# Keeping the last four blocks of a mixture of experts, not two, out of the sums in DRAM

## The reference

```python
logits = x @ gate_w                               # 2048 tokens, 8 experts
mult, sel = _sparse_mixer_routing(logits)         # two experts and two weights for each token
w = jnp.sum(mult[:, :, None] * (sel[:, :, None] == jnp.arange(E)[None, None, :]), axis=1)
h = jax.nn.silu(jnp.einsum('th,ehf->etf', x, w1)) * jnp.einsum('th,ehf->etf', x, w3)
out = jnp.einsum('etf,efh,te->th', h, w2, w)
...
x = _layernorm(x + _L0_ffn_ref(x, ...), axis=-1)
return x
```

## Time and profile before

| | us |
|---|---|
| median of 3 runs | 675.57 (674.59 to 675.78) |
| profiled execution | 674.35 |
| its span, first to last instruction | 672.7 |
| TensorE busy in the span | 580.6 (86%) |
| VectorE busy | 455.6 (68%) |
| ScalarE busy | 247.8 (37%) |
| GpSimd busy | 285.6 (42%) |
| mean granted TensorE clock | 0.935 of full speed |

### The profile page before, as it was taken

One profiled execution on the slowest core, in us unless ns is written; L12 is line 12 of the kernel. 1 busy time (PEld: TensorE's weight loads), 2 busy tenths in 40 slices (PEclk: granted clock), 3 DMA queues, 4 the chain that ended last, 5 costly groups with the idle time before them and its releaser, 6 DMA issues.

```text
span 672.7 us, 13915 instructions
## 1 busy us (share of the span) xinstructions
PE 580.6 (86%) x3498; PEld 452.7 (67%) x3499; DVE 455.6 (68%) x1363; ACT 247.8 (37%) x475; POOL 285.6 (42%) x208
## 2 busy tenths in 40 slices
PE   6999989699698867556998989999999999999940
PEld 2444568588366645444786878888888888888840
DVE  2566487956567778967775757768677777677751
ACT  3555540001676633224222414242332242422333
POOL 7100020002093447646651856719484185761142
PEclk9999999999889979557999989999999999999985
DMA  8999507201300106222367574856767467444453
GB/s 272 330 335 336 181 1 202 51 1 44 144 2 1 34 24 251 79 92 92 80 166 189 148 197 98 241 128 160 201 156 219 94 144 220 82 94 88 77 165 122
DMA packets 75514, 93.15 MB, mean 138 GB/s; under 512 B 15837, under 2 KB 70494, under 8 KB 72656
## 3 DMA queue, kind: packets, MB, share of 16 engines
q1 hardware_dynamic: 63808, 78.81, 40.0%
q0 software_dynamic: 6768, 9.32, 7.4%
q10 hardware_dynamic: 4896, 4.53, 2.7%
HBM read 42.67 MB, written 31.67 MB: 111 GB/s over the span
## 4 chain that ended last, share of the span: by engine, by line
PE 60%; DVE 17%; POOL 7%; ACT 5%; issue 5%; DMA 4%; SPq 1%; another core or an unknown queue 1%; ACTq 0%; POOLq 0%; DVEq 0%
PE bank L2382 23%; PE bank L2394 12%; PE bank L1952 8%; PE bank L2111 4%; POOL experts_w L859 2%; DVE region L1374 2%; DVE region L1372 2%; DMA xcol<-xcol 1%; PE bank L2002 1%; PE bank L1961 1%; ACT wstage L1242 1%; DVE small L1391 1%; PE bank L1968 1%; DMA wstage<-total 1%; PE bank L2279 1%
## 5 line engine op out<-in xcount | busy, mean ns | idle before, releaser
L2382 PE MATMUL bank<-experts_w,experts_x 128*128 (+1 forms) x864 | 216.9, 401 | 3.9 <-issue 3.9
L2382 PEld LDWEIGHTS bank<-experts_w,experts_x 128*128 128x128 f32 x864 | 158.2, 189 | 38.3 <-issue 5.1
L2394 PEld LDWEIGHTS bank<-experts_w 128*128 128x128 f32 x840 | 105.2, 191 | 5.1 <-issue 2.3
L2394 PE MATMUL bank<-experts_w 128*128 x840 | 106.3, 283 | 1.7 <-DVE region L1857 1.7
L907 POOL DMA_INDIRECT total<-region,rid x34 | 52.6, 1547 | 125.4 <-DVE region L1857 103.4
L1172 ACT ACTIVATE region<-bank 128x512 f32<-128x512 f32 x72 | 42.3, 597 | 129.7 <-PE bank L2382 119.4
L1833 DVE TENSOR_TENSOR xcol<-region,bank 128x512 f32<-128x512 f32 x72 | 49.1, 682 | 40.6 <-ACT region L1172 40.5
L778 POOL TENSOR_TENSOR small<-small 128x4 f32<-128x4 f32 (+5 forms) x20 | 25.7, 1288 | 102.9 <-DVE small L1383 84.1
L1178 ACT CAST experts_w<-bank 128x512 fp32r<-128x512 f32 x70 | 40.6, 587 | 72.3 <-DVE bank L1842 65.4
L1952 PE MATMUL bank<-xcol,region 128*128 128x512 f32 x128 | 58.8, 618 | 7.4 <-DMA xcol<-in_xT 5.8
L887 POOL TENSOR_TENSOR experts_w<-wstage,experts_w 128x2048 f32 x12 | 55.3, 4624 | 13.2 <-ACT experts_w L1196 13.2
(11 more groups left out here) (367 smaller groups left out, 914.8 us busy)
## 6 DMA issues: line engine op xcount, KB each, us to landing
wstage<-in_w_exp SPq DMA_DIRECT2D x18, 1024.0 KB, 5.2
xcol<-xcol SPq DMA_DIRECT2D x140, 128.0 KB
slots<-padrow SPq DMA_DIRECT2D x8, 2210.0 KB, 19.8
wstage<-in_w_exp SPq DMA_DIRECT2D x2, 3072.0 KB, 12.1
region<-slots ACTq DMA_DIRECT2D x34, 130.0 KB
xcol<-in_xT SPq DMA_DIRECT2D x4, 512.0 KB, 6.7
xtok<-in_x SPq DMA_DIRECT2D x1, 2048.0 KB, 13.1
region<-in_ctxT SPq DMA_DIRECT2D x1, 2048.0 KB, 8.0
```

Source lines behind the costliest of these rows:

```text
L2382: mm = pe.matmul(bank[2 * u + m][:, :], (xTh, xTl)[a][:, s, k, :], moving(off, w, m * KD * F + k * F + u * HALF, HALF), start=(k == 0 and ...
L2394: mm = pe.matmul(bank[into][:, 0:D], (high, low)[a][:, u, c, :], moving(off, w, 2 * KD * F + (4 * u + c) * D, D), start=(u == 0 and c == 0 ...
```

## The change

Four blocks, g - 2 to last, are kept out of the sums (`LATE`). So that all four are the last expert's, the number of its blocks is set to at least four; the others are then filled with empty rows. Reading `total` back depends only on the send of block g - 3. The reading of part 0 is issued by ScalarE inside its `last_pair`, that of the others by SyncE. GpSimd's `last_pair` has no sends and has four gathers, into four more tiles of `ya`. The statistics, shifts and norms of the first parts are written into the last pair of VectorE and ScalarE. The down product of g - 1 goes to bank 7 and that of last to bank 3, as banks 6, 7, 1 and 3 hold the four late products until they are added. Two more rows of weights and row numbers are kept (`weight_end`, `rid_end`), and the tiles of the small statistics have room for NT + LATE entries. At the end GpSimd sends the rows of four blocks in place of two. ScalarE's `high_up(g)` in the last pair is gone (no new expert can begin there).

```diff
-ENDS = ((0, 2), (2, 4), (6, 4), (10, 4), (14, 2))
+ENDS = ((0, 4), (4, 4), (8, 4), (12, 2), (14, 2))
+LATE = 4
...
-        ya = wstage[:, 0:NT * D].rearrange("p (i d) -> p i d", d=D)
+        ya = wstage[:, 0:(NT + LATE) * D].rearrange("p (i d) -> p i d", d=D)
...
```

SyncE (`sp`):

```diff
-            for s in range(2):
-                sp.wait_ge(y_sent[s], 8 * even + 16 * s)
-                sp.sem_inc(sp_gate, 1)
+            sp.wait_ge(y_sent[1], 8 * even)
+            sp.sem_inc(sp_gate, 1)
...
-            for u, (first, n) in enumerate(ENDS):
+            for u in range(1, len(ENDS)):
+                first, n = ENDS[u]
                 sp.dma_start(ya[:, first:first + n, :], rows_of(total, u)).then_inc(y_back[u], 16)
...
-            sp.wait_ge(rows_sent, 16 * 2)
+            sp.wait_ge(rows_sent, 16 * LATE)
```

GpSimd (`pool`):

```diff
-            all_pairs(pool, pair, pair)
-            last = pool.value_load(tab_n[0:1, 1:2], min_val=2 * SURE - 2, max_val=NB - 2) + 1
-            pool.wait_ge(xg_turned, last + 1)
-            pool.sem_inc(pool_gate, 1)
-            pool.wait_ge(meta_done, last + 1)
-            pool.sem_inc(pool_gate, 1)
-            pool.wait_ge(y_sent[1], 8 * (last + 1))
-            pool.sem_inc(pool_gate, 1)
-            pool.wait_ge(rid_end_done, 1)
-            for s in range(2):
-                pool.indirect_dma_start(out=xg[:, s, 0:D], out_offset=None, in_=total,
-                                        in_offset=bass.IndirectOffsetOnAxis(ap=rid_end[:, s:s + 1], axis=0)).then_inc(gathered[s], 16)
+            def last_pair(p):
+                pool.wait_ge(y_sent[1], 16 * p)
+                pool.sem_inc(pool_gate, 1)
+                pool.wait_ge(rid_end_done, 1)
+                for n in range(LATE):
+                    pool.indirect_dma_start(out=ya[:, NT + n, :], out_offset=None, in_=total,
+                                            in_offset=bass.IndirectOffsetOnAxis(ap=rid_end[:, n:n + 1], axis=0)).then_inc(gathered[n], 16)
+            all_pairs(pool, pair, last_pair)
             for first, n in ENDS:
                 rsqrt(n, first)
-            rsqrt(2, NT)
+            for k in range(0, LATE, 2):
+                rsqrt(2, NT + k)
             pool.wait_ge(out_done, 16 * len(ENDS))
-            pool.wait_ge(fin_done, len(ENDS) + 1)
-            for s in range(2):
-                pool.indirect_dma_start(out=out, out_offset=bass.IndirectOffsetOnAxis(ap=rid_end[:, s:s + 1], axis=0),
-                                        in_=xg[:, s, 0:D], in_offset=None, bounds_check=T - 1,
+            for n in range(LATE):
+                if n % 2 == 0:
+                    pool.wait_ge(fin_done, len(ENDS) + n // 2 + 1)
+                pool.indirect_dma_start(out=out, out_offset=bass.IndirectOffsetOnAxis(ap=rid_end[:, n:n + 1], axis=0),
+                                        in_=ya[:, NT + n, :], in_offset=None, bounds_check=T - 1,
                                         oob_is_err=False).then_inc(rows_sent, 16)
```

ScalarE (`act`):

```diff
+            def norm_rows(u, first, n, ends):
+                act.wait_ge(shift_done, u + 1)
+                for k in range(first, first + n):
+                    row = ya[:, k, :]
+                    ins = act.activation(row, row, ACT.Identity, bias=shift[:, k:k + 1], scale=rsy[:, k:k + 1])
+                if ends:
+                    ins.then_inc(fin_done, 1)
             def last_pair(p):
                 g = 2 * p
+                last = g + 1
                 for u in range(2):
                     silu(g, u)
+                act.wait_ge(y_sent[1], 8 * g)
+                act.sem_inc(act_gate, 1)
+                first, n = ENDS[0]
+                act.dma_start(ya[:, first:first + n, :],
+                              total[first * P:(first + n) * P, :].rearrange("(i p) d -> p i d", p=P)).then_inc(y_back[0], 16)
                 for u in range(2):
                     high_turned(g - 1, u)
-                high_up(g)
-                last = g + 1
                 silu(last, 0)
                 act.wait_ge(grouped[0], 32 * g + 64)
                 act.sem_inc(act_gate, 1)
                 plain(last, 0)
                 for u in range(2):
                     high_turned(g, u)
+                norm_rows(0, 0, 4, True)
                 silu(last, 1)
                 high_end(0)
                 plain(last, 1)
+                norm_rows(1, 4, 3, False)
                 high_end(1)
+                norm_rows(1, 7, 1, True)
             all_pairs(act, pair, last_pair)
-            for u, (first, n) in enumerate(ENDS):
-                act.wait_ge(shift_done, u + 1)
-                for k in range(first, first + n):
-                    row = ya[:, k, :]
-                    ins = act.activation(row, row, ACT.Identity, bias=shift[:, k:k + 1], scale=rsy[:, k:k + 1])
-                ins.then_inc(fin_done, 1)
...
+            for u in range(2, len(ENDS)):
+                norm_rows(u, *ENDS[u], True)
+            for k in range(0, LATE, 2):
+                norm_rows(len(ENDS) + k // 2, NT + k, 2, True)
```

VectorE (`dve`); the first line is in the building of the block tables, after L1763:

```diff
+            link(dve.tensor_scalar(nblk[:, E - 1:E], nblk[:, E - 1:E], float(LATE), None, ALU.max))
...
+            waiting = {}
+            def end_stats(u):
+                first, n = ENDS[u]
+                dve.wait_ge(y_back[u], 16)
+                waiting[u] = norm_stats(first, n, 1e-5, first, ya)
+            def end_shift(u):
+                first, n = ENDS[u] if u < len(ENDS) else (NT + 2 * (u - len(ENDS)), 2)
+                n = slice(first, first + n)
+                dve.wait_ge(rs_done, waiting[u])
+                dve.scalar_tensor_tensor(shift[:, n], mv[:, n, 0], -1.0, rsy[:, n], ALU.mult, ALU.mult).then_inc(shift_done, 1)
+            def keep_end(n, of):
+                dve.tensor_scalar(weight_end[:, n:n + 1], of[:, 1:2], 1.0, None, ALU.mult)
+                return dve.tensor_scalar(rid_end[:, n:n + 1], of[:, 0:1], 1.0, None, ALU.mult)
+            def late_rows(g, n, down_in):
+                dve.wait_ge(down_done, 2 * g + 2)
+                dve.wait_ge(gathered[n], 16)
+                link(dve.scalar_tensor_tensor(ya[:, NT + n, :], bank[down_in][:, 0:D], weight_end[:, n:n + 1], ya[:, NT + n, :],
+                                              ALU.mult, ALU.add))
             def last_pair(p):
                 g = 2 * p
                 last = g + 1
                 rows(last, 1)
                 middle(g, 0, 0)
-                keep_meta(g - 1, 1)
+                dve.wait_ge(meta_kept, g - 1)
+                keep_end(0, kept[:, 0])
+                dve.wait_ge(meta_done, g + 1)
+                keep_end(1, meta[:, 1, 3:5])
                 row_meta(last, 1)
+                keep_end(2, meta[:, 0, 3:5])
+                dve.wait_ge(meta_done, last + 1)
+                keep_end(3, meta[:, 1, 3:5]).then_inc(rid_end_done, 1)
                 middle(g, 0, 1)
...
-                weigh(g - 2, 0)
+                end_stats(0)
                 middle(last, 1, 0)
-                keep_meta(g, 0)
-                dve.wait_ge(meta_done, last + 1)
-                dve.tensor_copy(rid_end[:, 0:1], meta[:, 0, 3:4])
-                dve.tensor_copy(rid_end[:, 1:2], meta[:, 1, 3:4]).then_inc(rid_end_done, 1)
...
-                weigh(g - 1, 1)
+                end_shift(0)
+                end_stats(1)
                 middle(last, 1, 1)
-                keep_meta(last, 1)
-                for u in range(2):
-                    low_turned(last, u, bank[2 * u], endTh, endTl)
+                low_turned(last, 0, bank[0], endTh, endTl)
+                end_shift(1)
+                end_stats(2)
+                low_turned(last, 1, bank[2], endTh, endTl)
+                end_shift(2)
+                end_stats(3)
+                end_stats(4)
+                end_shift(3)
+                late_rows(g - 2, 0, 6)
+                late_rows(g - 1, 1, 7)
+                end_shift(4)
+                waiting[5] = norm_stats(NT, 2, 1e-5, NT, ya)
+                late_rows(g, 2, 1)
+                late_rows(last, 3, 3)
+                end_shift(5)
+                waiting[6] = norm_stats(NT + 2, 2, 1e-5, NT + 2, ya)
+                end_shift(6)
             all_pairs(dve, pair, last_pair)
-            for u in range(len(ENDS) + 2):
-                if u < len(ENDS):
-                    first, n = ENDS[u]
-                    dve.wait_ge(y_back[u], 16)
-                    norm_stats(first, n, 1e-5, first, ya)
-                elif u == len(ENDS):
-                    whole_rows(last - 1, 0, 1)
-                    whole_rows(last, 1, 6)
-                    norm_stats(0, 2, 1e-5, NT, xg)
...
```

TensorE (`pe`), in `last_pair`:

```diff
-                    down(g - 1, u, off, hTh, hTl)
+                    down(g - 1, u, off, hTh, hTl, 7)
...
-                    down(last, u, off, endTh, endTl, 6, g)
+                    down(last, u, off, endTh, endTl, 3)
```

More of the change, by code:

```diff
@@ L225, in decoder_kernel @@
         padrow = sb("padrow", ROW)
-        small = sb("small", 1017)
+        small = sb("small", 1037)
         at = [0]
@@ L249, in decoder_kernel @@
```

(28 more changed lines are left out.)

22 lines of the change are left out of this document (5 added, 17 removed).

## The result

The changed kernel takes 669.83 us (median of 13 runs, 665.50 to 672.14); the kernel before, over 13 runs beside it, 675.62 (670.36 to 677.19). The ratio is 0.9912, 95% interval 0.9892 to 0.9933: faster by 5.8 us, where 5.5 had been forecast (670.1). The profiled execution has a span of 668.6 us, against 672.7. Of all timed executions in this document one is left out as slow: 700.95 us at a clock of 0.814, of block_first, whose other three took 661.55 to 667.29 us.

A forecast was written before the change was run, and what follows sets the result against it. Bound: 26 us behind TensorE's end, set by the first read, the two engines' order and the sends. End 667.1 plus 0.17 gave span 667.3 against 672.7, 5.4 less; median 670.1 us, range 668.9 to 671.7.

The forecast's parts named there:

- The bound: End of the kernel: 26 us come after TensorE ends, and work there could lie beside TensorE, where VectorE and ScalarE have room.
- Start of the read: ScalarE in the last pair: block 31's sum lands at 628.95 us, and the first part's read is issued at 629.
- T: Landing of the first four tiles of `total`, when VectorE's statistics start: 634.1 us, bounds 632.9 and 635.7.
- the regrouping of block 34: SP's four copies before the last transposes: issued by 632.1 us, due at 636.65.
- The starving: Rival: block 34's regrouped rows land late, at 641.0 us for +4.3, or after 11.8 us for 677.4; chance 0.07.
- Every microsecond of T is one of the end: Crowding rival's rule: VectorE and ScalarE stand in line from T to X; T 637.2 gives end 3.1 later; chance 0.21.
- The two lines from there to X: VectorE and ScalarE in the last pair: four norms to 641.7 us, SiLU to 642.3, last low part to 646.75.
- X: End of the last low part, block 35: 646.75 us, 2.06 later than before, with TensorE ending near 648.4.
- Writes and sends: Kernel's end: last tiles written at 655.1 us (3.22), span ending 9.3 after plus two more sends at 1.36: 667.1.
- Signs of being wrong: T past 637; SP's parts issued before the regrouping lands and holding it; GpSimd's late powers (0.7 to 1.0 us) holding a shift.
- The sum: Whole kernel: span 667.3 us against 672.7, 5.4 less, and median 670.1; chance 0.55.
- the longer table chain: Start of the kernel: one more linked VectorE operation in the table chain, taken as +0.17 us.

The follow-up runs named there:

- block_first: Changed kernel with block 35's work ahead of the closing layernorm on VectorE and ScalarE; ratio to the kernel before 0.9878, tail 42.9 us.
- all_behind: Changed kernel with VectorE's statistics and shifts and ScalarE's norms of the 16 tiles behind the last pair again; tail 47.8 us.
- gathers_later: Changed kernel with GpSimd's four gathers waiting until block 34 has been transposed; tail 47.2 us.
- regroup_clear: block_first plus GpSimd's first power ahead of its gathers and SyncE's reads waiting for block 34's regrouping; 665.51 us, ratio to the kernel before 0.9896, tail 41.7.
- read_later: Changed kernel with ScalarE issuing the first part's read behind its two copies of block 33's turned rows; tail 44.1 us.
- two_sends: Changed kernel with GpSimd sending only the rows of blocks 34 and 35, leaving out 32 and 33; tail 41.8 us.
- bulk_later: Changed kernel with SyncE's reads of parts 1 to 4 waiting until block 34 has been transposed; tail 44.3 us.

## Why the prediction was right

**The bound.** That the 26 us behind TensorE were the place to gain, and that VectorE had room for a part of that work beside TensorE, held: with the statistics put back (all_behind) the tail is 47.8, with them 42.6.

**Start of the read and T.** 3.9 and 8.9 us after block 31's send were predicted, 3.8 and 9.0 came. The estimate between two bounds was good (5.2 us from issue to use for 0.52 MB). By the fit of the Trainium skill (DMA: Bandwidth & Descriptors, Anatomy of one DMA) it would be 3.2, an estimate for a transfer alone, and the page has the fit from transfers that GpSimd issues, while ScalarE issues this one; the measurement decides. Yet T hardly mattered, as it had 1.7 us of slack. SyncE's reads began at 10.4 (9.0 in the two other profiles), not at 6.9. Its last issue of the regrouping ends at 632.98 and its first read starts at 636.41; what it does in between stays open.

**The step that was mis-sized: the regrouping of block 34.** I had its landing due at 11.5 and not late; it landed at 13.4, 7.05 us from the start of the last issue. In the kernel before it was there by 10.2, as the transposes ran without a wait. The starving that stood among the rivals did occur, at 2.0 us instead of the 4.3 to 7.3 priced there (both prices run from 632.1, the end of the last issue; the 8.86 us of the earlier trace rows run from an issue's start, and the last one starts at 631.5, so they are 0.6 too high). The reads do it together: gathers away 0.3 to 0.9, SyncE's parts away 0.3, both away 1.5 or more. The Trainium skill (DMA: Bandwidth & Descriptors, Queues, rings and completion order) has all queues share the same engines in turn, and the runs agree: the copies, issued on SyncE's queue before its own reads, land 7.05 us from the start of their last issue, 6.20 when GpSimd's gathers come later (gathers_later), and at most 5.6 when SyncE's reads do too (regroup_clear). Whether its second half, the order of completion, adds to that, no run here separates. What the first read alone costs wasn't tried, as there was no run without it. Where nothing was altered ahead of it this landing still differs by up to 0.5 us (transposes at 13.5, and at 14.0 in block_first), so the single shares are no better than that. "Every microsecond of T is one of the end" was wrong in its subject: read_later gave 1.5 for 3.4. There the transposes' start and the tail both moved by 1.5. In regroup_clear 1.4 at the transposes gave 0.9.

**The two lines from there to X.** With the transposes 2.0 late, the SiLU came 1.8 and X 1.5 late: the steps between were a little shorter than summed. From X to the last tiles' shift the prediction takes 4.06 and 3.91 came (649.15 to 653.06); its own terms there add up to 3.89 (0.09, twice 1.13, 0.09, 1.30 and 0.15), so the terms were right and the addition was 0.17 too long.

**Writes and sends.** Here the error was given back. The first send starts 3.2 us after ScalarE's last norm of the tiles (28.1 to 31.4), where 4.1 had been summed from the 3.22 of the earlier trace rows and 0.86. The write lands 2.1 us after its issue, not 3.2, and it isn't what GpSimd waits for any more: that is VectorE's line through the late blocks, which the prediction had taken as covered. Sends follow each other by 1.27 to 1.36, where 1.36 was taken. The third send starts 1.5 us after the last late norms (32.5 to 34.0), where 2 had been summed, and a send needs 0.93 of that behind the norms (two_sends); so the added sends cost 0.7 to 0.8 in their own right though they stand on the path with 2.6.

**Signs of being wrong.** The prediction named three. The first, T past 637, didn't come. The second did: SyncE's parts are issued at 10.4, before the regrouping lands at 13.4, and bulk_later puts their hold at 0.3 us. The third did too: VectorE's last shift stands 0.81 us for GpSimd's late power (657.28; 0.75 in the kernel before, at 659.78), and the one of part 2 stands 0.24 (649.39). The time came out right although two of the prediction's own signs of being wrong were there; 0.3 and 0.81 us are small beside its range.

**The sum.** Tail 41.9 predicted, 42.5 measured: the gain in the tail is 4.97 us (47.51 less 42.54), not 5.6. The median moved by 5.8. What lies before the tail moves by more than this from run to run, so that the median agrees so closely is partly luck. For the same reason no run shows the 0.17 us taken for the longer table chain: the start of block 31's send alone differs by 5.3 us between two profiles of the changed kernel (626.06 and 620.77).

## What to carry to other kernels

When work is moved beside a busy engine, the order on the two helper engines becomes the path. Walk that line instruction by instruction, with every power or SiLU that one of them waits for: a wait of 5.37 us came out at the end with 4.6, while taking away one of 0.69 gained 0.1 to 0.2, as it uncovered the next (twice 0.53 us for GpSimd, then 1.39 for a write).

An early transfer isn't free because its own data come in time: look which transfers of the old critical work it runs beside. Here reads of up to 2.6 MB (20 tiles of 128 x 256) on three queues delayed 0.5 MB of copies that nobody had waited for before.

Undo the moved work and keep the early data: that one run showed which half of the change carried the gain.

## What the runs showed of the hardware

Three profiles of one and the same program spread over 5.2 us in span (668.6, 663.4, 666.5), while their tails agree within 0.1 (42.54, 42.63, 42.61). The difference lies in the middle of the program. Stages of the changed kernel's first profile, then of its second (columns as above):

```profile
100.00:200.00 100.00, 87.34 (x680) 65.72 (x680) 68.19 (x160) 25.95 (x63) 20.30 (x16) 0.91 0.26 75
...
300.00:340.00 40.00, 32.27 (x145) 25.85 (x146) 27.57 (x116) 11.51 (x11) 26.12 (x25) 0.79 0.28 84
...
400.00:620.00 220.00, 219.34 (x1259) 190.32 (x1258) 156.83 (x434) 75.95 (x105) 127.54 (x46) 1.00 0.62 152
```

```profile
100.00:200.00 100.00, 86.84 (x692) 65.80 (x691) 68.55 (x161) 26.76 (x66) 20.13 (x16) 0.95 0.26 75
...
300.00:340.00 40.00, 34.17 (x165) 27.45 (x165) 31.96 (x128) 13.89 (x15) 29.07 (x27) 0.85 0.37 97
...
400.00:620.00 220.00, 219.34 (x1260) 190.27 (x1259) 156.69 (x429) 76.48 (x106) 125.97 (x45) 1.00 0.61 149
```

From 400 us on both have a clock of 1.00 and the same busy time; between 100 and 200 us the granted clock is 0.91 in the one and 0.95 in the other, between 300 and 340 us 0.79 and 0.85. Such a mean lies between the two levels of 1.2 and 2.4 GHz: the clock was at the lower one for a larger or smaller part of the stretch. The mean over the span is 0.926, 0.943 and 0.936 in the three, and the one with the highest is the shortest. The 13 timed runs say the same: the four with a mean clock of 0.939 or more took 665.50 to 667.79 us, the other nine, at 0.933 or less, 669.16 to 672.14. That the clock makes the difference, and isn't lowered by what makes it, no run separates. In those stages TensorE has gaps (of the first 100 us shown 87 are busy with matmuls and 66 with weight loads). A change at the end of the program is therefore better judged by its tail, here within 0.1 us in three profiles, than by a handful of total times.

A transfer of 0.5 MB from SBUF to SBUF, issued in four pieces, landed at most 3.9 us from the start of its last issue in the kernel before (631.5 to 635.4, at a DMA share of 0.43 from 632 to 636), and 7.05 us from it in the changed kernel, when reads from DRAM on three queues ran beside it at a DMA share of 1.03 to 1.11.
